# Decay matrices from row loads and three groups of small products in a pipelined delta-rule kernel

## The reference

```python
q, k, v = silu(causal_conv(x @ W_qkvz))        # 4 taps for each channel
beta = sigmoid(b); g = -exp(A_log) * softplus(a + dt_bias)
for each token t, for each value head:
    S = S * exp(g_t)
    delta = (v_t - k_t @ S) * beta_t
    S = S + outer(k_t, delta)
    o_t = q_t @ S
out = rmsnorm(o * silu(z)) * norm_w @ W_out
```

## Time and profile before

| | us |
|---|---|
| median of 3 runs | 3131.32 (3124.35 to 3132.2) |
| the profiled execution | 3119.58 |
| its span in the profile | 3117.6 |
| PE, DVE, ACT, POOL busy | 2977.7, 2341.5, 1771.9, 1693.4 |
| granted clock of PE, mean | 0.979 of full speed |

### The profile page before, as it was taken

The page is one execution under the profiler, slowest core; times in us unless marked ns, Lnnn a source line. Parts: engine busy times, 40 slices in busy tenths (PEclk is TensorE's granted clock), DMA queues, the critical chain, the costliest instruction groups (busy, mean ns, idle before and its releaser), DMA issues. The chain is left out here.

```text
span 3117.6 us, 70222 instructions
## 1 busy us (share of the span) xinstructions
PE 2977.7 (96%) x23017; PEld 2174.3 (70%) x23017; DVE 2341.5 (75%) x4933; ACT 1771.9 (57%) x5794; POOL 1693.4 (54%) x3744
## 2 busy tenths in 40 slices
PE   5998699999999999999999999999999999978998
PEld 4556377777777777777777777777777777764655
DVE  3433588888888888888888888888888888746766
ACT  4322466666666666666666666666666666532332
POOL 2000466676666766676767666766766767610000
PEclk9999799999999999999999999999999999978999
DMA  3000111112112111111111212121111111210000
GB/s 85 1 1 14 27 44 37 44 37 45 42 44 46 40 44 42 44 37 45 37 44 37 47 42 50 39 48 38 44 37 44 37 44 37 46 38 4 7 7 14
DMA packets 447088, 113.77 MB, mean 36 GB/s; under 512 B 350528, under 2 KB 445872, under 8 KB 446704
## 3 DMA queue, kind: packets, MB, share of 16 engines
q1 hardware_dynamic: 446704, 108.99, 15.7%
HBM read 63.85 MB, written 45.09 MB: 35 GB/s over the span
## 5 line engine op out<-in xcount | busy, mean ns | idle before, releaser
L907 ACT ACTIVATE raw<-bank 128x512 f32<-128x512 f32 x256 | 153.3, 599 | 428.8 <-PE bank L680 423.4
L464 POOL TENSOR_TENSOR Tb<-Tb,btmp 64x14 f32<-64x14 f32 (+6 forms) x896 | 327.5, 365 | 70.9 <-POOL btmp L460 1.2
L1175 DVE SCALAR_TENSOR_TENSOR conv<-raw,ckq,conv 128x512 f32<-128x512 f32 x384 | 323.7, 843 | 24.2 <-ACT conv L908 13.2
L460 POOL TENSOR_TENSOR btmp<-Bk,Tb 64x14 f32<-64x14 f32 (+6 forms) x896 | 296.6, 331 | 65.6
L1175 DVE SCALAR_TENSOR_TENSOR conv<-raw,cv,conv 128x512 f32<-128x512 f32 x384 | 292.1, 761 | 13.8 <-ACT conv L908 2.7
L680 PE MATMUL bank<-xnT,wkq 128*128 128x512 f32 x512 | 254.8, 621 | 17.4 <-issue 11.8
L448 POOL TENSOR_SCALAR Tb<-Bk 64x256 f32<-64x256 f32 x64 | 73.7, 1151 | 341.2 <-DMA Bk<-blk_n 341.2
L680 PE MATMUL bank<-xnT,wv 128*128 128x512 f32 x512 | 248.8, 609 | 7.0 <-issue 4.7
L749 PE MATMUL bank<-wout_h,gT 128*128 128x256 f32 x1024 | 249.6, 387 | 1.3 <-ACT gT L927 1.2
L522 PE MATMUL bank<-S,ykq 128*128 128x256 f32 x1024 | 243.2, 379 | 5.8 <-issue 5.8
L852 ACT ACTIVATE sq_kq<-bank 128x128 bf16<-128x128 f32 x512 | 134.9, 278 | 194.6 <-PE bank L622 194.6
(11 more groups left out here) (350 smaller groups left out, 7543.3 us busy)
## 6 DMA issues: line engine op xcount, KB each, us to landing
blk_n<-N SPq DMA_DIRECT2D x128, 256.0 KB, 2.6
Tp<-blk_t SPq DMA_DIRECT2D x128, 128.0 KB, 2.9
Wp<-blk_w SPq DMA_DIRECT2D x128, 128.0 KB, 3.0
wkq<-in_L_attn_W_qkvz_dram SPq DMA_DIRECT2D x32, 128.0 KB, 2.4
wv<-in_L_attn_W_qkvz_dram SPq DMA_DIRECT2D x16, 256.0 KB, 3.1
Bk<-blk_n SPq DMA_DIRECT2D x64, 64.0 KB, 2.7
blk_t<-Tb SPq DMA_DIRECT2D x64, 64.0 KB, 2.5
blk_w<-Wb SPq DMA_DIRECT2D x64, 64.0 KB, 2.5
```

The source lines that it names most:

```text
L460: pool.tensor_tensor(tmp, Bk[:, j, j + 1:].unsqueeze(2).broadcast_to([64, 15 - j, j]), Tb[:, j, 0:j].unsqueeze(1).broadcast_to([64, 15 - j ...
L464: pool.tensor_tensor(Tb[:, j + 1:, 0:j], Tb[:, j + 1:, 0:j], tmp, ALU.subtract).then_inc(row_rdy, 1)
L907: act.activation(raw[h][:, j, :, 3:], bB[1 - j], ACT.Copy)
L1175: dve.scalar_tensor_tensor(out=conv[h][:, j], in0=raw[h][:, j, :, k:k + 256], scalar=cw[:, j, k:k + 1], in1=conv[h][:, j], op0=ALU.mult, o ...
```

## The change

1. *Decays from running sums.* The gate block keeps the running sum of g (kind CUM in place of G). It turns the sums, so that they lie as rows, and writes them to DRAM (`decay_rows`). In `delta_rule`, SP loads a step's rows onto all partitions (`decays`, 256 KB in SBUF for a step). ACT computes relu(c_i - row_j) in `clamp` and exp(-that) in `expo`. PE's `decay` and POOL's product for `gtri` are gone.
2. *Three groups of small products.* `w3` moves to the next slot (S_L + 1) and stands beside `x16`; `x64` follows `w1`; `w2` follows `w64`.
3. *Solve inside the first projection.* The two matmuls of `project(s, 0)` are split: the first ahead of `w64`, the second after `solve`.
4. *Orders.* ACT takes the evacuation of w64 (`wev64`) from DVE and has a new order. So has DVE (`add_w3` ahead of silu, `attention` ahead of `update`, the taps of both halves interleaved), and on POOL `step_gates` and `causal` stand first.

```diff
+                def decays(s):
+                    t = s.back(S_F - 2)
...
+                    free = held(sp, t.done(2))
+                    sp.wait_ge(m["made"], 2)
+                    sp.wait_ge(hd["rows_out"], 16)
+                    wait(sp, exp_rdy, free)
+                    sp.dma_start(rowb[t.c % 2][:].rearrange("p (b v) n -> p b (v n)", b=B),
+                                 rows[t.c, :, bass.ds(t.head(), 1), :].rearrange("b h n -> b (h n)").partition_broadcast(P)
+                                 ).then_inc(rowb_in[t.c % 2], 16)
 # SP
                 def body(s):
+                    decays(s)
                     weights(s)
                     base_out(s)
                     dump(s)
 # POOL
-                    wait(pool, dt_mm, t.done(1))
-                    pool.tensor_tensor(gtri[:], le4[:], gs[t.c][:, G, :].unsqueeze(2).broadcast_to([P, U, P]),
-                                       ALU.mult).then_inc(gtri_rdy, 1)
...
                 def body(s):
+                    step_gates(s)
+                    causal(s)
                     derive(s)
-                    causal(s)
                     halo(s)
                     base_rest(s)
-                    step_gates(s)
                     base_first(s)
                     out_scale(s)
 # PE
-                def decay(s):
...
-                    pe.matmul(bank[1][:], m["gt"][:], gtri[:].rearrange("p u n -> p (u n)"), start=True,
-                              stop=True).then_inc(dt_mm, 1)
...
 # w3: t = s.back(S_L + 1); w1 into bank 5, w2 into bank 4
 # w64:
+                    wait(pe, w3_rdy, done)
+                    wait(pe, w1_rdy, next_w1)
...
                 def body(s):
                     front_tp(s)
                     state_in(s)
-                    x64(s)
+                    w3(s)
                     x16(s)
-                    decay(s)
                     causal(s)
                     w1(s)
+                    x64(s)
+                    project(s, 0, (0,))
                     w64(s)
-                    project(s, 0)
+                    w2(s)
                     solve(s)
-                    w2(s)
+                    project(s, 0, (1,))
                     values(s)
                     apply(s)
-                    project(s, 1)
-                    w3(s)
+                    project(s, 1, (0, 1))
                     gated_tp(s)
                     zproj(s)
 # ACT
+                def clamp(s):
+                    t = s.back(S_F - 1)
...
+                    act.wait_ge(rowb_in[t.c % 2], t.pairs(16, 16))
+                    act.wait_ge(gs_rdy, t.done())
+                    for u in range(U):
+                        i = act.activation(rowb[t.c % 2][:, u, :], rowb[t.c % 2][:, u, :], ACT.Relu, scale=-1.0,
+                                           bias=gs[t.c][:, CUM, u:u + 1])
+                    i.then_inc(rel_rdy, 1)
...
-                    act.activation(ET[:], bU[1], ACT.Exp).then_inc(exp_rdy, 1)
+                    act.activation(ET[:], rowb[t.c % 2][:], ACT.Exp, scale=-1.0).then_inc(exp_rdy, 1)
...
+                def wev64(s):
...
+                    act.activation(Wf[0:64, :, 64:], bG[5][0:64], ACT.Copy).then_inc(w64_rdy, 1)
...
                 def body(s):
                     ztanh(s)
+                    expo(s)
                     norms(s)
                     silu(s)
                     from_state(s)
+                    normed(s)
                     xev64(s)
-                    expo(s)
-                    normed(s)
+                    wev64(s)
+                    kdec(s)
+                    vscale(s)
                     evac(s, 0)
-                    vscale(s)
-                    kdec(s)
+                    clamp(s)
                     evac(s, 1)
+                    gtev(s)
                     squares(s)
-                    gtev(s)
 # DVE
                     accumulate(s)
                     rhs(s)
                     xev16(s)
+                    add_w3(s)
+                    add_w1(s)
                     silu(s)
-                    add_w64(s)
-                    add_w1(s)
                     strict(s)
                     uscale(s)
                     add_w2(s)
+                    attention(s)
                     update(s)
                     output(s)
-                    attention(s)
-                    taps(s, 0)
-                    add_w3(s)
-                    taps(s, 1)
+                    taps(s)
 # the gate block, at its end
+                def gate_rows():
+                    pe.wait_ge(act_rdy, 5)
+                    for q in range(4):
+                        i = pe.transpose(psB[:, 0, q * P:(q + 1) * P], ab[:, q * P:(q + 1) * P], m["ident"][:])
+                    i.then_inc(cum_rdy, 1)
...
+                act.activation(turned, psB[:, 0, :], ACT.Copy).then_inc(turned_rdy, 1)
...
+                sp.dma_start(rows.rearrange("(q c) b h (v n) -> (c b h v) q n", q=4, v=2),
+                             turned.rearrange("p (q n) -> p q n", q=4)).then_inc(hd["rows_out"], 16)
```

More of the change, by code:

```diff
@@ L23 @@
 NKIND = 6
-G, BETA, NGAM, GAM, DEC, GLAST = range(NKIND)
+CUM, BETA, NGAM, GAM, DEC, GLAST = range(NKIND)
 UNIT = P * (P + 1)
@@ L106, in masks, with delta_rule @@
     return m
-def delta_rule(nc, ins, m, l2, hd, acc, xn, xnT, gates):
+def delta_rule(nc, ins, m, l2, hd, acc, xn, xnT, gates, rows):
     S_P, S_S, S_F, S_L, S_D, S_E = 0, 1, 2, 5, 6, 7
@@ L132, in delta_rule @@
         le4 = sb("le4", [P, U, P])
-        gtri = sb("gtri", [P, U, P])
+        rowb = [sb(f"rowb{r}", [P, U, P]) for r in range(2)]
         ET = sb("ET", [P, U, P])
@@ L547, in w1 @@
                     W = Wp[t.c // 2 % 2][:, t.c % 2]
-                    loaded, before, done = held(pe, t.pairs(32, 32)), held(pe, t.done(1)), held(pe, t.done())
+                    loaded, done = held(pe, t.pairs(32, 32)), held(pe, t.done())
                     pe.wait_ge(m["made"], 2)
@@ L667, in project @@
                     w = wv if t.c % 2 else wkq
[L668 to L671, removed]
-                    if j:
-                        wait(pe, vb_rdy, t.done(2))
-                        ends(pe, s, braw_rdy, t, 1)
-                    else:
-                        wait(pe, exp_rdy, t.done(2))
-                        ends(pe, s, araw_rdy, t, 1)
+                    if part[0] == 0:
+                        if t.c % 2:
+                            pe.wait_ge(wv_in, t.head(32, 32))
+                        else:
+                            pe.wait_ge(wkq_in, t.head(64, 64))
+                        if j:
+                            wait(pe, vb_rdy, t.done(2))
+                            ends(pe, s, braw_rdy, t, 1)
+                        else:
+                            wait(pe, zz_rdy, min(t.done(6), STEPS) if t.i is None else t.done(6))
+                            ends(pe, s, araw_rdy, t, 1)
                     q = t.c // 2
-                    for k in range(KT):
+                    for k in part:
                         i = pe.matmul(bank[1 - j][:], w[:, k, j * P:(j + 1) * P],
@@ L917, in xev64 @@
                     act.activation(Xs64[64:], bG[4][64:], ACT.Copy, scale=-1.0).then_inc(xs64_rdy, 1)
+                def wev64(s):
+                    t = s.back(S_L + 1)
+                    if not t.live:
+                        return
+                    act.wait_ge(w64_mm, t.done())
+                    act.activation(Wf[0:64, :, 64:], bG[5][0:64], ACT.Copy).then_inc(w64_rdy, 1)
                 def gtev(s):
@@ L984, in _ @@
                 dve.wait_ge(setup, 5)
-                def add_w64(s):
-                    t = s.back(S_D)
-                    if not t.live:
-                        return
-                    dve.wait_ge(w64_mm, t.done())
-                    dve.tensor_copy(Wf[0:64, :, 64:], bG[5][0:64]).then_inc(w64_rdy, 1)
                 def accumulate(s):
@@ L1571, in _, with routed_loop @@
                 v.wait_ge(r_rd, 1)
-def routed_loop(nc, ins, m, r, x, xn, xnT, gates):
+def routed_loop(nc, ins, m, r, hd, x, xn, xnT, gates, rows):
     w1T, w2A, b1c, b2r, b1a, b1d, b2m, topw, wsum, sel, z1T, rb, wba, dtb, alog, xnS = (r[k] for k in (
@@ L1827, in gate_end @@
                     v.wait_ge(act_rdy, 5)
+                    for b in range(B):
+                        v.tensor_copy(into(CUM, b), of(ab[:], b))
+                    v.wait_ge(act_rdy, 6)
                     v.tensor_scalar(gates[:, :, NGAM, :], gates[:, :, GAM, :], -1.0, None, ALU.mult)
```

79 lines of the change are left out of this document (42 added, 37 removed).

## The result

| | us | ratio to before (95%) |
|---|---|---|
| predicted | 3078 (2985 to 3140) | |
| before, 4 runs | 3131.76 (3124.35 to 3137.64) | |
| after, 4 runs | 3271.59 (3270.43 to 3272.77) | 1.0448 (1.0425 to 1.047) |

The change makes the kernel slower by 140 us. The forecast was faster, and its range does not hold the time. The granted clock is 0.98 as before, so it is not the clock.

A forecast was written before the change was run, and what follows sets the result against it. PE bound the kernel before; after the change a two-slot ring of POOL, transfers and DVE would bind at 36.5 us a pair. Slot 18.67 to 18.25 saves 53: 3119.6 - 53 + 1.3 = 3068, plus 10 gives 3078 (2985 to 3140).

The forecast's parts named there:

- ACT's walk: ACT's slot: clamp ends at 13.3, PE has the second projection ready at 13.5, so clamp's place is covered by 0.2 us.
- only changes order: DVE: gives up one copy of a 64x256 block and otherwise changes order; 89% of a 17.4 us slot.
- a sign of being wrong: PE's waits standing elsewhere: at w64 for ACT's xev64, or at the half projection for wv.
- The decay product: PE: removing decay takes 0.97 us off each slot, 18.54 to 17.57.
- Three groups of small products: PE: four groups taking 3.49 us become three at 3.35, bounds 3.49 and 3.1; 0.14 us saved a slot.
- clamp: ACT: four added activations of 128x128, 1.15 us together.
- The ring: POOL, transfers and DVE over two slots: dependent work binding at 36.5 us a pair, against PE's 34.9.
- rival 2: Ring at 37.1 to 37.5 a pair: stalls give back all, no change, about 3125; chance 0.09.
- slow `pow`: POOL's base rows: a pow of 2.03 us for 1.03; three tenths of 1.3 add 0.4 a pair.
- SP: Row load on SP's queue delays later weights: 0.1 us a slot, bounds 0 to 1.5 in one slot of eight.
- The routed block: Added transposes, activations, copies and rows' write at the block's end: 1.3 us once (0 to 4).
- Rival 3, POOL's lock: POOL's rows and DVE's taps lock each other out: ring 38.0, slot 19.0, 3173; slower, chance 0.16 with late rows counted in.

The follow-up runs named there:

- e4: Kernel before with only ACT's order edited to kdec, vscale, first evacuation: 3314.17 us, ratio 1.0647.
- e1: Changed kernel with eight buffers for kd in place of four: 3203.75 us, ratio 1.0285.
- e2: Changed kernel with ACT's order alone edited to vscale, first evacuation, kdec, clamp, four buffers kept: 3206.23 us, ratio 1.0301.
- e5: e2 with attention put behind the output on DVE: 3189.22 us, ratio 1.0203.
- e6: e5 with SP's weights also put ahead of decays: 3160.8 us, ratio 1.011.
- e9: e6 with clamp moved to the end of ACT's slot: 3130.98 us, ratio 1.0021.
- e8: Kernel before with decays from row loads only, old orders and groups, clamp and decays last on their queues: 3152.04 us, ratio 1.0072.
- experiment 3: The runs on clamp and the regrouping: e9 against e6, 3130.98 us, and e8 against the kernel before, 3152.04 us.
- e10: e9 with wv and cv loaded one slot earlier: 3138.87 us, ratio 1.006.
- e11: e8 with wv and cv loaded one slot earlier, everything computed: 3094.22 us, ratio 0.9907.
- e18: e11 with expo right behind ztanh on ACT and causal ahead of derive on POOL: 3114.29 us, ratio 0.9978.
- e15: e11 with uscale ahead of strict on DVE in even slots: 3148.26 us, ratio 1.0075.
- e3: Changed kernel with SP's weights ahead of decays: 3251.88 us, ratio 1.0439.

## Why the prediction was wrong, point by point

- **The step that failed is ACT's walk**: "vscale follows values at 9.8 to 11, first evacuation 12.1, clamp 13.3 ... Covered, by 0.2 us". It summed the work ahead of each part and never asked what the first part in the new order waits for. `kdec` stood ahead of `vscale`, and its wait for the up product holds vb until 1518.85, so that PE loses 1.53 us a slot where the walk had none. e4 shows the order alone to cost 199 us; e1 and e2 show that it is the wait (8 buffers do as much as another place).
- **Four losses stood one behind the other.** Behind the vb wait lay the gated transposes' (0.92: `attention` waits likewise, and `w3` was their cover), then gT's (0.6: `clamp` between the evacuations), and beside them the weights behind the rows' load. Each edit gave only what the next one left: e2, e5, e6, e9 stand 3.0, 2.0, 1.1 and 0.2% above before. The prediction gave "0.2 us" of cover to clamp's place; it was short by 0.6. Its sentence on DVE, "only changes order", was the same mistake as ACT's: it is the wait that moved.
- **What the prediction named as a sign of being wrong** was "if the waits stand elsewhere", at w64 or the half projection. They stood elsewhere, but at other places still.
- **The decay product** was the right term, but too large: 17.57 predicted without it, 17.77 measured in e8's clean slots. Its 0.97 us were taken as coming back whole, and 0.76 did; `w1` lost its cover and the causal product its place behind a large product (experiment 3).
- **Three groups of small products** were to save 0.14. They took some 0.05 more (3.54 for 3.49). By the Trainium skill (TensorEngine Tiling (Array Packing), Tiling Modes, Key Properties) one group less is one drain less; no gain from it is seen in this sum. The split of `project(s, 0)` costs 0.09: its halves take 1.05 and 0.86 to the next start (1510.96 to 1512.01, 1514.21 to 1515.07), the whole took 1.82 before (1521.04 to 1522.86). And with the half projection moved ahead of `w64`, only `w2` covers Wf's evacuation before `solve`: the wait for Wf, 0.27 in every slot. Clean slots are 18.0 us in e9 and 17.77 in e8: 0.23 more, or 29 us in 127 slots, near the size of this wait. e10 and e11, which both have the early load, stand at 3138.87 and 3094.22, but they differ in more than regrouping and split: in e10 `expo` and POOL's `causal` also stand early, which cost e11 some 20 us in e18, and other orders of ACT, DVE and SP are the change's. So how much of the 45 us is the regrouping's isn't shown.
- **clamp** was 1.15 us for four activations and measured 1.33.
- **The ring** was right in its mechanism and in the places where PE meets it (Us in even slots, Tp in odd ones, as forecast). This was seen in e9 and e11, not in the kernel after, whose other waits hid it. Its size was low: 36.5 a pair predicted. In e9 a pair takes 2 x (2698.0 - 323.7) / 127 = 37.4, which is rival 2's "37.1 to 37.5", and e9 is at before's level, as that rival had it; in e11 it is 2 x (2666.1 - 322.9) / 127 = 36.9. The slow `pow` was counted with three even slots in ten; in e11 24 of 49 have it (600 to 2400 us).
- **SP**: "I take 0.1 a slot". In the kernel after it is about that: the waits for ckq and cv are 12.9 us in 91 slots, 0.14 each. But with shorter slots they grow, to 25.8 us in e5 and 35.4 in e8. The bounds were 0 to 1.5 us in one slot of eight; in e8 that slot took up to 6 us more. There the row load is slow itself (5.6 us), wv, issued right behind it, lands after 4.9 us for 3.1, and PE's wait is followed by the lower clock.
- **The routed block** was to cost 1.3 us (0 to 4). The first front transposes stand 5.3 us later.
- **Rival 3, POOL's lock**, predicted slower but for a reason that isn't there: the operations that end each row (L475) average 363 ns in the page of after, where the same group had 365 before, and the time was lost at ACT's waits. By the Trainium skill (SBUF — State Buffer, Who interferes with whom) they would have grown under DVE's work; their mean did not, but e18 agrees with the rule from the other side, as DVE's taps took 1.20 us for 0.78 under POOL's masking. The prediction's pair of rows (0.77 for 0.64) could not price it: in the slow slot, too, DVE was at its taps (from 1529.08) when the 0.64 began.

## What to carry to other kernels

When a part is moved in an engine's order, look up what it waits for before adding up its work: a ring of n buffers whose consumer runs n slots later makes its producer wait on the same slot, harmless at the end of an order and costly at its head. When such a wait is undone, expect another part of the same change behind it, so undo until a single part is left; here that part alone, with one load moved to fit (e11), was faster than before. Work taken away is also cover taken away, so look at what the next instruction waited for behind it. And where a ring of work over two slots is a few tenths from binding, PE can meet it at more than one place, and an edit at one of them only moves the wait.

## What the runs showed of the hardware

The granted clock fell after some single waits of PE: in e8 to 0.52 after 2.25 us without work. In e15, with a wait of 3.38 us for Tp ahead of 1514.27, it is 0.50, that is the lower of the two levels (windows of PE, columns as in e8's):

```profile
1513.50:1518.00 4.50, 3.73 (x34) 0.50 0.66 155
1518.00:1531.00 13.00, 13.00 (x111) 0.95 0.27 52
```

But not every such wait is followed by it. In e5, a wait of 2.38 us for cv ahead of 1218.45 left the clock at 1.00, and one of 2.35 ahead of 1833.68 was followed by 0.50:

```profile
1218.00:1226.00 8.00, 7.28 (x59) 1.00 0.21 42
1834.80:1838.00 3.20, 3.14 (x33) 0.50 0.36 71
```

Waits of 0.3 to 1.5 us in every slot of the kernel after left it at 1.00. And the load that repeats rows onto all partitions takes 5.0 us for 256 KB, where N's write of the same size takes 2.9. What counts for the weights is whether it is issued right ahead of them: then wkq lands after 4.3 us (after) and also after 4.8 in e8, where the load ends SP's slot and the next slot begins with the weights; where it is issued behind them, after 2.2 (e3) and 2.3 (e6).

The two parts of the split projection, alike in size, took 1.05 us to the next start with small products (64x64) ahead and behind, and 0.86 with large ones on both sides; the causal product took 1.06 with small products on both sides (after) and 0.95 with them only behind it (before). So the border between small and large products has a price of some 0.1 us in these rows.
